# A gated delta-rule layer with experts on one core: a loop body of six chunks instead of one, squares summed on ScalarE from transposed tiles, and another order of the work

## The chip, the cores and the metric

The kernel runs on one core of a Trainium2 chip. TensorE (PE) multiplies, VectorE (DVE), ScalarE (ACT) and GpSimd (POOL) do the element-wise work, SyncE (SP) issues the DMAs. Each engine takes its own instructions in the order in which they stand; they wait for one another by semaphores. The metric is the device time of one execution in microseconds, the median of the runs shown. Data are float32; some products take rounded float32 or bfloat16 parts.

## The reference, cut to what matters

The input is 2 sequences of 2048 tokens with 256 features. Each layer norm, the attention-like part, the second norm and the experts are all computed:

```python
mixed = hidden_states @ Wqkv.T + bqkv               # 4096 channels: q 8x128, k 8x128, v 16x128
z = hidden_states @ Wz.T + bz
beta = sigmoid(hidden_states @ Wb.T + bb)
g = -exp(A_log) * softplus(hidden_states @ Wa.T + ba + dt_bias)
y = depthwise_causal_conv(mixed, conv_w, taps=4) + conv_b
q, k, v = split(silu(y))
q, k = repeat(q, 2, heads), repeat(k, 2, heads)      # 8 -> 16 heads
q = q * rsqrt(sum(q * q) + 1e-6) * 128 ** -0.5
k = k * rsqrt(sum(k * k) + 1e-6)
for t in tokens:                                     # per head, state is 128 x 128
    state = state * exp(g_t)
    delta = (v_t - k_t @ state) * beta_t
    state = state + outer(k_t, delta)
    out_t = q_t @ state
core = out * rsqrt(mean(out * out) + 1e-6) * norm_w * silu(z)
x = x + layernorm(core @ Wout.T + bout)
x = x + layernorm(shared(x_n) + top8_of_16_experts(x_n))   # x_n = layernorm(x)
```

## The kernel before, in words

The tokens are cut into 32 chunks of 128. The recurrence is taken chunk by chunk: within a chunk of a head it is a triangular system whose inverse is built (16 by 16 blocks on GpSimd, then three doubling levels on TensorE and a correction), and the state S of 128 x 128 a head is carried on. The 16 heads of a chunk go in four groups of four; **a group of a chunk is an item**, so there are 128 items. A group has two pairs of q and k tiles and four v tiles.

The work is a pipeline over items. In item w = (t, g) each engine does, in one fixed order: projection, convolution taps and SiLU of the item three ahead (a, "new"); k-q products, sums of squares, decays and the triangle of the item two ahead (f, "front"); the doubling levels of the item one ahead (v, "invert"); state products, solve and new state of w itself ("state"); gate, norm and output projection of the item before (u, "post"). Four functions more hang on certain groups: `chunk_front` makes the normed input and gates of the next chunk (groups 0 and 1), `experts` runs the expert part of the chunk before (norms in group 0; hT, ffn1, G0 in group 1; G1, G2 in group 2; G3, laT, ffo in group 3; the products D0 to D3 in between).

The order of this is written out by hand in a function `item(w, stages)` on each engine, four of them (TensorE's at L702, ScalarE's at L981, VectorE's at L1317, and those of GpSimd and SyncE). `run` calls them: t = -1 and t = 0 as straight code, t = 1 to 30 in a loop (`eng.Fori(1, chunks - 1)`, L313) whose body holds the four items of one chunk, t = 31 and 32 as straight code. Values that semaphores are waited for depend on the loop's register.

PSUM has eight banks with fixed uses: bF0 and bF1 take the projections of q, k and of v (and bF0 half of G, bF1 the gate's projection z); bQ the k-q products, the exponents and the inversion's Q; bXT the sums of squares, the transposed k, the transposed parts and the inversion's transposed X; bX v's transposes and X; bS and bD the state products, solve and new state; bB, by turns in the order of `B_ORDER`, core transposes, output projection and the experts' products.

The places that the change touches, in the order of one item on the data's way: ScalarE's `silu` makes QK; `square_qk` (L842) squares its four tiles of 128 x 128 into Sq at the end of the item; in the next item TensorE's `ss` (L492) multiplies each with a column of ones, which leaves four sums a token in bXT; VectorE's `squares` (L1138, L1140) adds the epsilon into Sse and makes Epq; `ktr` (L499), behind it on TensorE, transposes the two k tiles into the same bank, which ScalarE's `keys` (L865) copies to Kn. ScalarE's `key_norm` (L859, L861) takes logarithm and root of Sse; GpSimd makes the decay exponents with it in nine small steps (L1455 to L1471, the last write Parts); TensorE's `parts_t` (L505) transposes them, ScalarE copies (PartsT), TensorE's `exponents` (L517 to L521) spreads them over bQ, and ScalarE's `decays` (L887) makes Ex, from which GpSimd makes the triangle Ln and AT. The k-q products (`kkq`, L484) go to bQ. `correct` (L580) ends the inversion of w, `refined` (L1162) copies it to Tt, `solve` (L602) uses it. `update_s` (L1186) writes S for two heads; `ks_qs` (L594, L595) of the second pair waits for the first pair's update.

Of the kernel before, what the change touches and what calls it, by code (L numbers as in the profile page):

```python
# [39 lines left out]
P = 128  # L40
# [60 lines left out]
def layer_kernel(nc, x, wqkv, conv, wz, wba, rows, cols, wout, shared1, wlat, shared2, wup, rw, rw2,  # L101
# [6 lines left out]
    with ctx:  # L108
# [63 lines left out]
        Sq = sb("Sq", [P, 2 * GK, P])  # L172
        Sse = sb("Sse", [P, 2 * GK])
# [71 lines left out]
        def heads(bank):  # L245
# [6 lines left out]
            proj_full=2, z_full=1, kkq_full=1, ss_full=1, ktr_full=1, partsT_full=1, vtr_full=1, exp_full=1,  # L252
# [53 lines left out]
        def run(eng, item):  # L306
# [135 lines left out]
        def _(pe):  # L442
# [45 lines left out]
            def ss(f):  # L488
                pe.wait_ge(sem["xt_done"], at("xt_done", ahead(f, -2)))
                pe.wait_ge(sem["sq_done"], at("sq_done", f))  # L490
                for i in range(2 * GK):
                    last = mm(bXT[:, i:i + 1], Sq[:, i, :], ones[:, 0:1], start=True, stop=True)  # L492
                last.then_inc(sem["ss_full"], 1)

            def ktr(f):
                t, g = f
                pe.wait_ge(sem["sse_done"], at("sse_done", f))
                for kh in range(GK):
                    last = nc.tensor.transpose(heads(bXT)[:, kh, :], QK[:, g, 2 * kh + 1, :], ident)  # L499
                last.then_inc(sem["ktr_full"], 1)  # L500

            def parts_t(f):
                pe.wait_ge(sem["kn_done"], at("kn_done", f))
# [198 lines left out]
            def item(w, stages):  # L702
# [3 lines left out]
                if state:  # L706
                    ks_qs(w, 0)
                if new:
                    proj(a, 0, 0)
                if c and g == 1:  # L710
                    chunk_front(t + 1, "ba")
                if new:
                    proj(a, 0, 1)
                if front:
                    ss(f)
                if state:
                    correct(w)
                if front:
                    kkq(f)
                    ktr(f)  # L720
                if state:
                    solve(w, 0)
                if new:
                    proj(a, 1, 0)
                if front:
                    parts_t(f)
                if post:
                    core_t(u)
                if front:
                    vtr(f)  # L730
                    exponents(f)
# [3 lines left out]
                if new:  # L735
                    proj(a, 1, 1)
                if e and g == 1:
                    experts(t - 1, "hT", 0)
                if invert:
                    invert_begin(v, front)  # L740
                    invert_q(v, 0)
                if c and g == 1:
                    chunk_front(t + 1, "gc")
                if state:
                    ks_qs(w, 1)
                if e and g == 1:
                    experts(t - 1, "ffn1", 0)
                if invert:
                    invert_xt(v, 0)
                    invert_x(v, 0)  # L750
                if e and g == 3:
                    experts(t - 1, "G", 3, a if new else (chunks - 1, GROUPS - 1))
                if e and g == 2:
                    experts(t - 1, "G", 1, a if new else (chunks - 1, GROUPS - 1))
                if invert:
                    invert_q(v, 1)
                if state:
                    solve(w, 1)
                if post:
                    out_proj(u)  # L760
                if invert:
                    invert_xt(v, 1)
                    invert_x(v, 1)
                if e and g == 2:
                    experts(t - 1, "D", 1)
                if state:
                    az(w, 1)
                if invert:
                    invert_q(v, 2)
                if e and g == 1:  # L770
# [851 lines left out]
```

## Time and profile before

| what | value |
|---|---|
| median of 3 runs | 3548.47 us |
| lowest and highest | 3543.68 and 3554.87 us |
| the profiled execution's own time | 3551.05 us |
| its span, first to last instruction | 3549.2 us |
| mean granted clock of TensorE | 0.963 of 2.4 GHz |
| busy: PE, DVE, ACT, POOL | 3291.3, 2714.1, 2423.9, 2145.0 us |
| DMA | 143.89 MB, mean 41 GB/s |

How to read it: the span is one execution with a profile. Busy time of PE is modelled for pipelined products, and PEld is the load of the stationary operand that goes with each product and overlaps the one before; the distance between the starts of two PEld groups is the time that TensorE gives to the first. The slices of the page show TensorE at 90% or more from the second to the last but two, so the kernel is even over its length, and one chunk inside it can stand for all. A wait is put down to what released it; "issue" means that the profile shows nothing that did.

### The profile page before, as it was taken

The numbers are of one execution on the slowest core, as the hardware profiler recorded it, in microseconds if no ns is written. First come the engines' busy times: TensorE is split into PE (matmuls) and PEld (weight loads), VectorE is DVE, ScalarE is ACT, GpSimd is POOL, SyncE is SP. The second block draws the span as 40 slices with busy tenths as digits, with TensorE's granted clock in tenths as the row PEclk, the third lists the DMA queues.
The fourth block names the chain that finished last, engine by engine and source line by source line (L and its number), as shares of the span: only waits on it lengthen the run. The fifth ranks groups of instructions, "written<-read, shape, count | busy, mean of one in ns | idle before, by whom it ended". The sixth has DMA issues, their size and how long they took to land.

```text
span 3549.2 us, 86916 instructions
## 1 busy us (share of the span) xinstructions
PE 3291.3 (93%) x23968; PEld 2920.5 (82%) x24096; DVE 2714.1 (76%) x8720; ACT 2423.9 (68%) x5922; POOL 2145.0 (60%) x5380
## 2 busy tenths in 40 slices
PE   4999999999999999999999999999999999999986
PEld 4888888888888888888888888888888888888875
DVE  4777777877777777778787777777778777778773
ACT  3777667767767766777776777676677676677662
POOL 3766666666656656666666666666666666566660
PEclk8999999999999999999999999999999999999996
DMA  4111111111111111111111111111111111111110
GB/s 173 42 37 40 41 34 39 38 36 36 41 37 33 41 39 36 35 42 35 36 45 36 34 42 35 36 42 39 34 42 35 36 37 44 35 35 43 36 41 4
DMA packets 424188, 143.89 MB, mean 41 GB/s; under 512 B 211168, under 2 KB 421664, under 8 KB 423200
## 3 DMA queue, kind: packets, MB, share of 16 engines
q1 hardware_dynamic: 423712, 139.83, 15.1%
q14 instruction: 457, 3.74, 0.4%
q8 instruction: 19, 0.31, 0.0%
HBM read 93.11 MB, written 46.66 MB: 39 GB/s over the span
## 4 chain that ended last, share of the span: by engine, by line
PE 71%; ACT 13%; issue 8%; DVE 4%; POOL 2%; DMA 2%; DVEq 0%; SPq 0%; ACTq 0%; POOLq 0%
PE bF L464 9%; PE bB L635 6%; PE bQ L545 5%; PE bXT L553 4%; ACT L809 4%; PE bF L475 3%; PE bB L691 3%; PE bS L602 3%; PE bF L477 3%; PE bB L685 3%; PE bD L617 3%; PE bS L610 3%; PE bS L594 3%; PE bX L558 2%; PE bD L595 2%
## 5 line engine op out<-in xcount | busy, mean ns | idle before, releaser
L1103 DVE SCALAR_TENSOR_TENSOR Y<-bF,Cv,Y 128x127 f32<-128x127 f32 (+2 forms) x3072 | 852.0, 339 | 33.9 <-ACT Y L826 29.0
L464 PE MATMUL bF<-XnT,Wqkv 128*128 128x128 f32 x4096 | 556.5, 286 | 0.5 <-ACT XnT L945 0.5
L464 PEld LDWEIGHTS bF<-XnT,Wqkv 128*128 128x128 f32 x4096 | 530.1, 202 | 9.5 <-issue 2.1
L826 ACT ACTIVATE Y<-bF,Cv 128x128 f32<-128x128 f32 x1024 | 387.7, 456 | 151.4 <-PE bF L464 107.4
L896 ACT ACTIVATE XiT<-bXT 128x512 fp32r<-128x512 f32 x384 | 228.7, 596 | 296.2 <-PE bXT L553 295.1
L1531 POOL TENSOR_TENSOR Tp<-Tp 32x64 f32<-32x64 f32 (+2 forms) x768 | 361.3, 470 | 60.2
L1146 DVE TENSOR_TENSOR Qi<-bQ,Cf 128x512 fp32r<-128x512 f32 x384 | 264.0, 687 | 97.6 <-PE bQ L545 96.4
L809 ACT ACT_TABLE_LOAD x257 | 329.7, 1283 | 5.4 <-PEq L1615 0.7
L553 PE MATMUL bXT<-Qi,Xi 128*128 128x128 f32 x1536 | 301.9, 319 | 2.4 <-DVE Qi L1146 2.4
L553 PEld LDWEIGHTS bXT<-Qi,Xi 128*128 128x128 f32 x1536 | 222.1, 192 | 96.2 <-DVE Qi L1146 47.3
L1524 POOL TENSOR_TENSOR Tp<-Yb,Tm 32x64 f32<-32x64 f32 (+1 forms) x384 | 276.9, 721 | 30.1
L1524 POOL TENSOR_TENSOR Tp<-Cb,Yb 32x64 f32<-32x64 f32 (+1 forms) x384 | 274.0, 713 | 32.7 <-POOL Yb L1533 5.0
L1425 POOL TENSOR_TENSOR Ln<-Ex,KKQ 128x512 f32<-128x512 f32 x128 | 163.9, 1281 | 209.5 <-ACT Ex L887 140.3
L1539 POOL TENSOR_TENSOR Yb<-Cb,Cf 32x8 fp32r<-32x8 f32 x128 | 25.6, 200 | 392.6 <-DMA Cb<-DL 392.6
L545 PE MATMUL bQ<-XiT,LnR 128*128 128x128 f32 x1536 | 240.7, 280 | 19.4 <-ACT XiT L896 19.4
L545 PEld LDWEIGHTS bQ<-XiT,LnR 128*128 128x128 f32 x1536 | 211.8, 191 | 47.6 <-ACT XiT L896 28.7
L635 PE MATMUL bB<-Wout,CoT 128*128 128x256 f32 x1024 | 244.2, 382 | 0.9 <-ACT CoT L932 0.8
L1169 DVE SCALAR_TENSOR_TENSOR R<-bS,Sc,Vs 128x128 f32<-128x128 f32 x512 | 154.2, 342 | 98.5 <-issue 77.7
L903 ACT ACTIVATE Xi<-bX 128x512 fp32r<-128x512 f32 x384 | 226.4, 590 | 2.8 <-PE bX L564 2.3
L1458 POOL TENSOR_TENSOR HG<-LnbG,Lnk 128x4 f32<-128x4 f32 x128 | 25.7, 201 | 325.2 <-ACT Lnk L859 325.2
L635 PEld LDWEIGHTS bB<-Wout,CoT 128*128 128x128 f32 x1024 | 186.2, 192 | 21.4 <-ACT CoT L932 1.1
L602 PE MATMUL bS<-R,Tt 128*128 128x128 f32 x1024 | 179.3, 301 | 22.9 <-DVE Tt L1162 22.8
(198 smaller groups left out, 9272.2 us busy)
## 6 DMA issues: line engine op xcount, KB each, us to landing
DL<-Ln SPq DMA_DIRECT2D x128, 256.0 KB, 2.2
XiT<-DX SPq DMA_DIRECT2D x128, 256.0 KB, 2.8
Xi<-DX SPq DMA_DIRECT2D x128, 256.0 KB, 3.2
DX<-Yb SPq DMA_DIRECT2D x256, 32.0 KB, 1.8
Xf<-x SPq DMA_DIRECT2D x32, 128.0 KB, 3.2
Wqkv<-wqkv SPq DMA_DIRECT2D x4, 1024.0 KB, 17.1
Cb<-DL SPq DMA_DIRECT2D x128, 32.0 KB, 1.9
Xr<-x SPq DMA_DIRECT2D x32, 128.0 KB, 2.9
```

The costliest lines, as they stand in the source:

```text
L464: last = mm(bank[:, i, :], Wqkv[:, k, c:c + P], XnT[:, k, :], start=(k == 0), stop=(k == KT - 1))
L545: last = mm(heads(bQ)[:, h, :], LnR[:, h, :], XiT[:, h, :], start=True, stop=True)
L553: last = mm(heads(bXT)[:, h, :], Xi[:, h, :], Qi[:, h, :], start=False, stop=True, skip_group_check=True)
L602: last = mm(heads(bS)[:, i, :], Tt[:, 2 * p + i, :], R[:, i, :], start=True, stop=True)
L635: last = mm(bB[:, 0:HID], CoT[:, h, :], Wout[:, g * GH + h, :], start=(h == 0), stop=(h == GH - 1))
L809: nc.scalar.add_instruction(mybir.InstLoadActFuncSet(name=nc.get_next_instruction_name(), act_func_set_id=TABLES[name], engine=mybir.Engin ...
L826: last = op(Y[:, tile, :], bank[:, i, :], ACT.Identity, scale=c[:, TAPS - 1:TAPS], bias=c[:, TAPS:TAPS + 1])
L896: op(XiT[:, :, :], heads(bXT), ACT.Copy).then_inc(sem["xt_done"], 1)
L1103: last = stt(y, bank[:, i, 0:P - shift], Cv[:, g * TILES + tile, n:n + 1], y, ALU.mult, ALU.add)
L1146: tt(Qi[:, :, :], heads(bQ), level, ALU.mult).then_inc(sem["q_done"], 1)
L1524: then(tt(view(Tp[:, :], p * m ** 3, [[m * m, m], [m, m], [1, m]]), pair(left, p), pair(right, p), ALU.mult))
L1531: then(tt(lo, lo, hi, ALU.add))
```

## The change

Four edits.

- **The loop's body** holds six chunks (24 items) and is run 5 times, instead of one chunk run 30 times. `chunks - 2` is 30, and six is the first of 6, 5, 3, 2, 1 that divides it. In the built program TensorE's body has 3814 instructions instead of 647, ScalarE's 1697 instead of 283, VectorE's 2236 instead of 393, GpSimd's 2015 instead of 345.
- **Sums of squares**: `ss` is gone, and so is the squaring of QK as a whole at the end of `activated`. `ktr` transposes all four tiles, q and k, and waits for SiLU and for the bank. At the head of the item ScalarE squares each transposed tile from PSUM and sums it along the free axis with the instruction's accumulator into Ssq. `squares` on VectorE reads Ssq. `parts_t`, which overwrites the bank, waits for the squares too.
- **The order** of the items is written anew on TensorE, ScalarE and VectorE.
- `B_ORDER` has gc ahead of hT.

```diff
-            with eng.Fori(1, chunks - 1) as t:
-                for g in range(GROUPS):
-                    item((t, g), "cafispe")
+            steps = next(n for n in (6, 5, 3, 2, 1) if (chunks - 2) % n == 0)
+            with eng.Fori(0, (chunks - 2) // steps) as i:
+                for k in range(steps):
+                    for g in range(GROUPS):
+                        item((i * steps + k + 1, g), "cafispe")
...
-            def ss(f):
-                pe.wait_ge(sem["xt_done"], at("xt_done", ahead(f, -2)))
-                pe.wait_ge(sem["sq_done"], at("sq_done", f))
-                for i in range(2 * GK):
-                    last = mm(bXT[:, i:i + 1], Sq[:, i, :], ones[:, 0:1], start=True, stop=True)
-                last.then_inc(sem["ss_full"], 1)
-
             def ktr(f):
                 t, g = f
-                pe.wait_ge(sem["sse_done"], at("sse_done", f))
-                for kh in range(GK):
-                    last = nc.tensor.transpose(heads(bXT)[:, kh, :], QK[:, g, 2 * kh + 1, :], ident)
+                pe.wait_ge(sem["xt_done"], at("xt_done", ahead(f, -2)))
+                pe.wait_ge(sem["silu_done"], at("silu_done", f, 1))
+                for i in range(2 * GK):
+                    last = nc.tensor.transpose(heads(bXT)[:, i, :], QK[:, g, i, :], ident)
                 last.then_inc(sem["ktr_full"], 1)
...
             def square_qk(f):
-                act.wait_ge(sem["silu_done"], at("silu_done", f, 1))
-                act.wait_ge(sem["ss_full"], at("ss_full", ahead(f, -1)))
-                op(Sq[:, :, :], QK[:, f[1], :, :], ACT.Square).then_inc(sem["sq_done"], 1)
+                act.wait_ge(sem["ktr_full"], at("ktr_full", f))
+                act.wait_ge(sem["sse_done"], at("sse_done", ahead(f, -1)))
+                for i in range(2 * GK):
+                    last = op(Sq[:, i, :], heads(bXT)[:, i, :], ACT.Square, accum_out=Ssq[:, i:i + 1])
+                last.then_inc(sem["sq_done"], 1)
...
-                dve.wait_ge(sem["ss_full"], at("ss_full", f))
+                dve.wait_ge(sem["sq_done"], at("sq_done", f))
                 dve.wait_ge(sem["lnk_done"], at("lnk_done", ahead(f, -1)))
-                ts(Sse[:, :], bXT[:, 0:2 * GK], L2_EPS, None, ALU.add).then_inc(sem["sse_done"], 1)
+                ts(Sse[:, :], Ssq[:, :], L2_EPS, None, ALU.add).then_inc(sem["sse_done"], 1)
...
                 if front:
-                    ss(f)
+                    kkq(f)
...
+                if e and g == 3:
+                    experts(t - 1, "D", 2)
```

TensorE at the head of an item, here group 0, before (lines with ISA or REGISTER_ALU only set up waits and are left out by the dots; S are the state products, Wqkv the projections, Sq the sums of squares, bX<-Xi,Qi the correction):

```order
...
L594 MATMUL bS<-S,QK 128x256
L595 MATMUL bD<-S,QK 128x256
...
L464 MATMUL bF<-XnT,Wqkv 128x128 x8
...
L492 MATMUL bXT<-Cf,Sq 128x1 x4
...
L580 MATMUL bX<-Xi,Qi 128x128 x4
...
L484 MATMUL bQ<-QK 128x256 x2
L499 MATMUL bXT<-Cf,QK 128x128 x2
...
L602 MATMUL bS<-R,Tt 128x128 x2
L464 MATMUL bF<-XnT,Wqkv 128x128 x4
...
L505 MATMUL bXT<-Ch,Parts 128x128
```

And now:

```order
...
L592 MATMUL bS<-S,QK 128x256
L593 MATMUL bD<-S,QK 128x256
...
L487 MATMUL bQ<-QK 128x256 x2
...
L467 MATMUL bF<-XnT,Wqkv 128x128 x4
...
L496 MATMUL bXT<-Cf,QK 128x128 x4
L578 MATMUL bX<-Xi,Qi 128x128 x4
L467 MATMUL bF<-XnT,Wqkv 128x128 x4
...
L467 MATMUL bF<-XnT,Wqkv 128x128 x4
...
L600 MATMUL bS<-R,Tt 128x128 x2
L467 MATMUL bF<-XnT,Wqkv 128x128 x4
...
L503 MATMUL bXT<-Ch,Parts 128x128
```

The k-q products moved ahead of the projections, the transposes ahead of the correction, and all four parts of the projection now stand before the transposed parts; in groups 2 and 3 a product D stands before and behind the correction besides.

ScalarE at the head of the same item, before:

```order
...
L859 ACTIVATE Lnk<-Sse 128x2
L861 ACTIVATE Rki<-Lnk 128x2
...
L826 ACTIVATE Y<-bF,Cv 128x128 x4
L865 ACTIVATE Kn<-bXT 128x256
...
L910 ACTIVATE Qg<-bD,Sc 128x128 x2
L915 ACTIVATE Z<-bS 128x256
L874 ACTIVATE PartsT<-bXT 128x128
```

And now:

```order
...
L840 ACTIVATE Sq,Ssq<-bXT 128x128 x4
...
L908 ACTIVATE Qg<-bD,Sc 128x128 x2
...
L857 ACTIVATE Lnk<-Sse 128x2
L859 ACTIVATE Rki<-Lnk 128x2
...
L823 ACTIVATE Y<-bF,Cv 128x128 x4
L863 ACTIVATE Kn<-bXT 128x256
L913 ACTIVATE Z<-bS 128x256
L872 ACTIVATE PartsT<-bXT 128x128
```

The four squares and the scaling of the queries now stand ahead of the key norms.

VectorE in the same item, before (Y the taps, O and S the updates):

```order
...
L1138 TENSOR_SCALAR Sse<-bXT 128x4
L1140 TENSOR_SCALAR Epq<-Sse 128x2
...
L1162 COPY Tt<-bX 128x512
...
L1103 SCALAR_TENSOR_TENSOR Y<-bF,Cv,Y 128x127 x4
...
L1103 SCALAR_TENSOR_TENSOR Y<-bF,Cv,Y 128x126 x4
L1178 TENSOR_TENSOR O<-Qg,bS 128x256
L1186 SCALAR_TENSOR_TENSOR S<-S,Sc,bD 128x128 x2
...
L1103 SCALAR_TENSOR_TENSOR Y<-bF,Cv,Y 128x125 x4
```

And now:

```order
...
L1137 TENSOR_SCALAR Sse<-Ssq 128x4
L1139 TENSOR_SCALAR Epq<-Sse 128x2
...
L1161 COPY Tt<-bX 128x512
...
L1102 SCALAR_TENSOR_TENSOR Y<-bF,Cv,Y 128x127 x4
...
L1102 SCALAR_TENSOR_TENSOR Y<-bF,Cv,Y 128x126 x4
...
L1102 SCALAR_TENSOR_TENSOR Y<-bF,Cv,Y 128x125 x4
L1177 TENSOR_TENSOR O<-Qg,bS 128x256
L1185 SCALAR_TENSOR_TENSOR S<-S,Sc,bD 128x128 x2
```

The third set of taps moved ahead of the updates of O and S.

## Rows read from the trace of the kernel before

**Rows 1.** The page, busy us, share of the span, instructions of each engine.

```profile
PE 3291.3 (93%) x23968; PEld 2920.5 (82%) x24096; DVE 2714.1 (76%) x8720; ACT 2423.9 (68%) x5922; POOL 2145.0 (60%) x5380
```

**Rows 2.** Windows: stretch, its us, busy us of each engine, PEclk, DMA.

```profile
199.08:224.82 25.74, 23.80 (x168) 20.84 (x169) 21.53 (x77) 18.21 (x50) 17.00 (x43) 1.00 0.17 43
224.82:250.78 25.96, 25.55 (x201) 23.34 (x201) 20.68 (x73) 18.91 (x48) 16.62 (x43) 1.00 0.14 36
250.78:276.63 25.85, 25.66 (x206) 23.11 (x205) 19.80 (x60) 19.37 (x46) 16.64 (x43) 1.00 0.14 36
...
1026.98:1058.34 31.36, 28.05 (x187) 24.61 (x187) 22.30 (x66) 19.07 (x46) 16.67 (x43) 0.89 0.15 39
1058.34:1082.91 24.57, 23.07 (x167) 20.23 (x166) 21.55 (x78) 18.36 (x51) 16.89 (x43) 1.00 0.16 42
...
3387.80:3413.24 25.44, 25.03 (x187) 22.07 (x187) 21.88 (x66) 18.63 (x47) 16.72 (x43) 1.00 0.16 41
```

**Rows 3.** SyncE's stores of results, instructions of the loop, first and last start.

```profile
L394 SPq MOVE out<-Yo x30: 29/29/29, 297.0 to 3407.7; - x30
```

**Rows 4.** Waits: us in total, times, longest us.

```profile
DVE R L1169 <- issue: 77.7, 29, 3.1
...
PE bXT L499 <- DVE Sse L1138: 65.3, 29, 2.6
```

**Rows 5.** Windows behind the jump at 1046 us, columns as above.

```profile
1050.00:1052.00 2.00, 2.00 (x9) 2.00 (x10) 1.51 (x5) 1.09 (x4) 1.71 (x9) 0.50 0.08 18
```

**Rows 6.** Timeline, TensorE's loads in an item's head: start, us, engine, line.

```profile
1016.39 0.42 PEld L594 LDWEIGHTS bS<-S,QK 128*128 128x128 f32 x2
...
1017.27 1.97 PEld L464 LDWEIGHTS bF<-XnT,Wqkv 128*128 128x128 f32 x16
...
1019.16 0.97 PEld L492 LDWEIGHTS bXT<-Cf,Sq 128*128 128x128 f32 x8
...
1020.05 0.53 PEld L580 LDWEIGHTS bX<-Xi,Qi 128*128 128x128 f32 x4
...
1020.50 0.74 PEld L484 LDWEIGHTS bQ<-QK 128*128 128x128 f32 x4
...
1021.26 0.36 PEld L499 LDWEIGHTS bXT<-Cf,QK 128*128 128x128 f32 x2
...
1021.58 0.53 PEld L602 LDWEIGHTS bS<-R,Tt 128*128 128x128 f32 x4
...
1023.03 0.42 PEld L624 LDWEIGHTS bB<-Cf,O 128*128 128x128 f32 x4
...
1026.30 0.19 PEld L535 LDWEIGHTS bXT<-XiT,IdR 128*128 128x128 f32 x1
```

**Rows 7.** Timeline, the other engines in the same stretch.

```profile
1016.82 0.69 DVE L1148 TENSOR_TENSOR Qi<-bQ,Cf 128x512 fp32r<-128x512 f32 x1 [0.64 <-PE bQ L573]
...
1020.26 0.16 DVE L1138 TENSOR_SCALAR Sse<-bXT 128x4 f32<-128x4 f32 x1 [2.23 <-PE bXT L492]
...
1020.76 0.69 DVE L1162 COPY Tt<-bX 128x512 f32<-128x512 f32 x1
...
1020.83 1.50 ACT L826 ACTIVATE Y<-bF,Cv 128x128 f32<-128x128 f32 x4
...
1022.23 0.20 POOL L1471 TENSOR_TENSOR Parts<-HGf,Cf 128x8 bf16<-128x8 f32 x1
...
1022.48 0.65 ACT L910 ACTIVATE Qg<-bD,Sc 128x128 f32<-128x128 f32 x2
...
1023.10 2.26 DVE L1103 SCALAR_TENSOR_TENSOR Y<-bF,Cv,Y 128x127 f32<-128x127 f32 x8
...
1025.71 0.61 DVE L1186 SCALAR_TENSOR_TENSOR S<-S,Sc,bD 128x128 f32<-128x128 f32 x2
```

**Rows 8.** Groups of ScalarE by form: busy us, mean ns, idle before.

```profile
L859 ACT ACTIVATE Lnk<-Sse 128x2 f32<-128x2 f32 x128 | 25.5, 200 | 106.4 <-DVE Sse L1138 105.2
...
L977 ACT ACTIVATE LaT<-bB 128x128 f32<-128x128 f32 x32 | 8.9, 277 | 26.1 <-PE bB L695 26.1
```

More of the change, by code:

```diff
@@ L707, in item @@
                     ks_qs(w, 0)
+                if front:
+                    kkq(f)
                 if new:
                     proj(a, 0, 0)
[L710 to L711 removed]
+                if front:
+                    ktr(f)
+                if e and g == 2:
+                    experts(t - 1, "D", 0)
+                if state:
+                    correct(w)
+                if e and g == 3:
+                    experts(t - 1, "D", 2)
                 if new:
                     proj(a, 0, 1)
[L714 to L720 removed]
+                    proj(a, 1, 0)
                 if state:
@@ L734, in item @@
                     new_state(w, 0)
-                if new:
-                    proj(a, 1, 1)
+                if c and g == 1:
+                    chunk_front(t + 1, "gc")
+                if invert:
+                    invert_begin(v, front)
+                    invert_q(v, 0)
+                if state:
+                    ks_qs(w, 1)
                 if e and g == 1:
@@ L985, in item @@
                 if front:
+                    square_qk(f)
+                if state:
+                    query_state(w, 0)
+                if front:
                     key_norm(f)
@@ L1015, in item @@
                     experts(t - 1, "G", 1)
+                if e and g == 1:
+                    experts(t - 1, "ffn1", 0)
+                if state:
+                    query_state(w, 1)
+                    solved(w, 1)
                 if invert:
                     inverse(v, 0)
-                if state:
-                    solved(w, 1)
                 if c and g == 0:
@@ L1038, in item @@
                     experts(t - 1, "laT", 0)
+                if e and g == 2:
+                    experts(t - 1, "G", 2)
                 if new:
@@ L1322, in item @@
                     right_side(w, 0)
-                if e and g == 2:
-                    experts(t - 1, "D", 0)
-                if front:
-                    squares(f)
-                if new:
-                    ended(a)
-                if state:
-                    refined(w)
                 if post:
@@ L1333, in item @@
                 if front:
+                    squares(f)
+                if state:
+                    refined(w)
+                if new:
+                    ended(a)
+                if e and g == 3:
+                    experts(t - 1, "D", 2)
+                if e and g == 1:
+                    experts(t - 1, "hn", 0)
+                if front:
                     products(f)
+                if new:
+                    taps(a, 0, 2)
                 if c and g == 1:
                     chunk_front(t + 1, "sp")
+                if e and g == 2:
+                    experts(t - 1, "D", 0)
                 if new:
-                    taps(a, 0, 2)
                     taps(a, 0, 1)
-                if e and g == 1:
-                    experts(t - 1, "hn", 0)
+                    taps(a, 0, 0)
                 if state:
@@ L1344, in item @@
                     update_s(w, 0)
+                if c and g == 0:
+                    chunk_front(t + 1, "norm")
                 if new:
-                    taps(a, 0, 0)
                     tails_out(a, 0)
+                if invert:
+                    mask_q(v, 0)
                 if c and g == 1:
                     chunk_front(t + 1, "gc")
-                if invert:
-                    mask_q(v, 0)
-                if c and g == 0:
-                    chunk_front(t + 1, "norm")
+                if new:
+                    first_tokens(a, 0)
                 if state:
```

141 lines of the change are left out of this document (61 added, 80 removed), and 4 rows, old and new, of the table B_ORDER.

## The prediction

> **What bounds the kernel now.** I read the page first: TensorE is busy 93% of the span [rows 1], the others 60 to 76%, so the first question is where TensorE does not do useful work. The means of the page hide that, so I cut the span into items (four make a chunk of 128 tokens) at the DMA that carries an item's triangle out, and asked for the busy time of each stretch [rows 2]. Three kinds of stretch appear. In straight code (the first pass through the loop's body, the way out of the loop, and all items that lie inside an iteration) an item takes 25.44 to 25.96 us and the granted clock is 1.00. A stretch with the jump back to the top of the body in it takes 31.36 us, at a mean clock of 0.89, and the item behind it is a little shorter, 24.57 us. Three stretches of the first iteration, 25.74, 25.96 and 25.85, and the way out of the loop, 25.44, are together a chunk without a jump: 102.99 us. The iterations as they are: the stores of the results run from 297.0 to 3407.7 us in 30 iterations [rows 3], so 3110.7 / 29 = 107.27 us each.
>
> The difference, 4.28 us, is the price of one jump. The waits show its parts: 29 times VectorE stood before its first instruction of the body, 77.7 / 29 = 2.7 us, with nothing that released it; 29 times TensorE then waited for VectorE, 65.3 / 29 = 2.3 us [rows 4]. Behind that pause the granted clock is 0.50 (1.2 instead of 2.4 GHz) for some microseconds [rows 5]. A part of the loss is caught up in the next item, which is why I take the period and not the single stretch: 31.36 - 25.44 would say 5.9.
>
> Within straight code TensorE is the bound almost alone. Interval less busy time in the four stretches is 0.41 + 1.94 + 0.41 + 0.19 = 2.95 us of 102.99 [rows 2]. So its work is 100.0 us a chunk, and its stalls 3.
>
> **The change, part by part. The body of six chunks** removes jumps: 29 before, 4 after (5 iterations). 25 x 4.28 = 107 us. What each engine issues for a chunk stays about the same, and the straight parts of before show that code without a jump is supplied in time. A remark on the four that stay: the trace shows that TensorE itself began the next body without a pause at the jump (it waited only for VectorE), with a body of 647 instructions. The Trainium skill (Runtime: NRT & Kernel Launch, Instruction fetch mechanics) gives TensorE room for 2048 instructions and says that a taken branch to a target outside what is held stalls for a fetch. The new body has 3814 on TensorE, so by the page its jump would stall too; if that costs what VectorE's does, 4 x 2.7 = 11 us more, an estimate that no run here shows yet and that the sum leaves out.
>
> **Sums of squares.** On TensorE the four products with a column of ones go: they hold its load slot from 1019.16 to 1020.05, 0.89 us. The two transposes of k (1021.26 to 1021.58, 0.32) become four; four such transposes are 0.42 in the row of L624 [rows 6]. Gain 0.89 + 0.32 - 0.42 = 0.79 us an item, 3.1 a chunk: work 100.0 - 3.1 = 96.9 us. VectorE now reads four numbers a partition from SBUF instead of PSUM, which I cost at nothing.
>
> On ScalarE one squaring of 512 columns, off the path at the end of an item, becomes four of 128 columns read from PSUM with an accumulator, and they stand at the head of the item behind the transposes, on the path to the key norms. No row has the accumulator. The nearest rows are four instructions of 128 columns from PSUM in 1.50 us (L826) [rows 7] and one alone in 0.28 (L977) [rows 8]. From below 4 x 0.28 = 1.1 us; from above 1.5 plus 0.2 each if reading the accumulator is a small instruction of its own (a logarithm of two columns is 200 ns) [rows 8], 2.3. I take 1.5, the row with the same shape and source. The Trainium skill (ScalarE: Activation LUTs, What ACT_TABLE_LOAD costs) would have an instruction without pointer operands at 186 + 107 ns and 93 ns of overlap, so 0.9 us for the four, an estimate; the chain below would then be 0.6 us shorter in each item.
>
> **The order.** I walk the head of the new order with the durations of the old one, from the load of the state products at 1016.39 as zero [rows 6, 7]. TensorE: state products to 0.88. Then the k-q products, which stood behind ss: they write bQ, which VectorE's last mask of the item before must have read, and that ended at 1017.51, +1.12. So they start at 1.2 (**stall 0.3**) and end at 1.96 (0.76 long). One half of a projection (0.95) to 2.9, four transposes to 3.3. ScalarE can square from about 3.5 (a reader followed the last load by 0.2 at ss, 1020.05 to 1020.26) to 5.0; Sse at 5.2; Tt, 0.5 behind it in the old order and 0.4 in the new, from 5.6 to 6.3. TensorE meanwhile has the correction (0.45) and two halves (1.89): 5.65. In items 0 and 1 of a chunk it then waits for Tt until 6.35 (**stall 0.7**). In items 2 and 3 the products D stand there as cover and hide it. Key norms, exponents: from Sse to the last Parts were 2.17 us (1020.26 to 1022.43); ScalarE's scaling of the queries (L910, 0.65) now stands in front of the key norms, so they come at 5.2 + 2.17 + 0.45 = 7.8 (0.2 of the 0.65 run while Sse is made), and TensorE is there at 7.75; it waits a little for them, and again for ScalarE's copy, which has four taps (1.50) in front: **stall 0.35** together. Head: 1.35 us in items 0 and 1, 0.65 in 2 and 3.
>
> What comes later: the taps of q and k begin when ScalarE has done query scaling, key norms (two small ones, 0.45) and its own four taps, 5.0 + 0.65 + 0.45 + 1.5 = 7.6; before they began at 6.7 (1023.10). The new order puts all three sets (2.26 / 2 = 1.13 each) ahead of the update of O and S, before it was two. So S is updated at 7.7 + 3.4 + 0.4 + 0.6 = 12.1; before 1026.32, +9.9. TensorE's head took 9.91 (to the load at 1026.30), now 9.9 - 0.8 + 1.35 = 10.5 (much the same in items 2 and 3, where the products D fill the gap); with two copies into PSUM and the first inversion product, 0.9, it stands before the second pair of state products at 11.4 and waits for S: **stall 0.7** in every item. Queued behind that wait is all of the inversion chain.
>
> Sum of the walk for a chunk: 2 x 1.35 + 2 x 0.65 + 4 x 0.7 = 6.8 us. Of today's 3 us the order should take away the wait before the turned blocks, since z's second half now lies in between, and leave about 0.9: 7.7 us. That is a ceiling for the price of 1.5 us, since in it every engine keeps its old lateness, while ScalarE, with 19 of 25.9 us busy [rows 2], would be ahead by what it no longer does at the item's end. The floor is today's 3 us. A chunk is then 96.9 + 3.0 = 99.9 to 96.9 + 7.7 = 104.6 us, against 102.99. I take the middle, 102.3, because the two ends are worth the same to me: - 0.7 us a chunk.
>
> **Sum**, on the profiled execution's span of 3549.2 us, with 31 chunks' worth of full items: 3549.2 - 107 - 31 x 0.7 = 3420. The run lay 1.85 us above its span (3551.05), and 2.6 above the median of the three runs, so on the median's scale this is 3420 less 1: **about 3420 us**.
>
> **The rivals.** (a) The order hides its own waits, and all the work taken from TensorE is time: 99.9 us a chunk, 3549 - 107 - 31 x 3.1 = 3346. For it: VectorE stands 2.23 us waiting for ss in the item shown [rows 7], so there is slack to reorder in; against it the walk above. (b) The walk in full: 104.6 us a chunk, + 1.6 x 31 = 50, so 3492. For it: the S update and Tt are hard dependencies of the same item. (c) Slower than before: the accumulating squares are dear. They lie on the chain transposes, squares, Sse, Tt, taps, S, so each 0.1 us of them is 0.1 an item, 0.4 a chunk. With the walk in full the whole gain is gone when a chunk is 102.99 + 107 / 31 = 106.4 us, that is 1.8 / 4 = 0.45 us an item over the walk: squares of 1.95 us for the four. At the upper bound of 2.3 it is 0.8 an item, 107.8 a chunk: 3442 + 149 = 3591. (d) The jumps left become dearer, or more of the loss is recovered today than I see: at most some 10 to 20 us; it goes into the range. (e) The change does nothing for the jumps, because the straight code is not fed in time: then 29 stretches at 0.89 would be replaced by pauses elsewhere. The first iteration and the prologue speak against it, 0.02 of chance.
>
> **How the numbers follow.** Middle case, 3375 to 3460: 0.45. (a), 3335 to 3375, and somewhat under it where today's 3 us shrink too: 0.24. (b), 3460 to 3535: 0.20. (c) with (e): 0.11, of which 0.08 ends beyond + 0.3%, the rest within. A measurement of this kernel can tell about 0.3%, 10.6 us, from no change: that is 3538 to 3559. So faster 0.88, same 0.04, slower 0.08. For 8 in 10 the range takes in (a), the middle and the most of (b): 3335 to 3515.
>
> **What would show it.** Right for the jump: 4 times instead of 29 an unreleased pause of VectorE at the head of the body, the clock at 1.00 between, and straight items. Right for the squares: their four near 1.5 us, starting at 3.5 after the item's start. Right for the walk: waits of the solve for Tt and of the second state products for S in most items; if they are absent, (a) holds. Wrong: squares over 1.9 us, a chunk inside the body longer than 103 us with TensorE's idle time ahead of the solve or the state products, or a clock that falls within the body because those stalls add up.

## The result and the profile after

| | before | after |
|---|---|---|
| median | 3549.74 us (4 runs) | 3455.02 us (4 runs) |
| lowest and highest | 3543.68, 3554.87 | 3447.76, 3462.44 |
| profiled execution, its span | 3551.05, 3549.2 us | 3456.82, 3455.0 us |
| mean granted clock | 0.963 | 0.980 |

The ratio is 0.9736, 95% interval 0.9722 to 0.9751: 2.6% faster, 95 us between the medians. The forecast was 3420 us, with a range of 3335 to 3515.

The page of the changed kernel, to set beside [rows 1]:

```profile
span 3455.0 us, 84800 instructions
...
PE 3197.1 (93%) x23200; PEld 2796.3 (81%) x23328; DVE 2756.8 (80%) x8720; ACT 2502.6 (72%) x6818; POOL 2151.3 (62%) x5380
```

TensorE has 768 products fewer (1024 of `ss` gone, 256 transposes more), ScalarE 896 instructions more, seven an item. Four squares instead of one are only three of them; the other four are read-outs of the accumulator (below).

The windows, cut at the same DMA as [rows 2]: first the stretch with a jump, then the four items of a straight chunk behind it.

```profile
792.94:825.06 32.12, 26.42 (x183) 23.11 (x182) 22.14 (x66) 19.51 (x54) 16.67 (x43) 0.95 0.16 41
825.06:849.96 24.90, 22.70 (x156) 19.47 (x158) 22.23 (x74) 19.08 (x57) 17.20 (x43) 1.00 0.17 43
849.96:876.20 26.24, 25.61 (x196) 22.95 (x195) 21.69 (x75) 19.53 (x55) 16.67 (x43) 1.00 0.14 35
876.20:902.16 25.96, 25.37 (x198) 22.41 (x198) 19.73 (x61) 19.98 (x53) 16.67 (x43) 1.00 0.15 36
902.16:927.76 25.60, 24.33 (x179) 21.44 (x179) 21.67 (x65) 19.23 (x54) 16.71 (x43) 1.00 0.18 46
```

This straight chunk takes 102.70 us (102.6 to 103.8 in the others, 102.9 in the mean; one, with an item of 28.9 us, takes 105.2) and TensorE is idle for 0.6 to 2.2 us in each item, 4.7 in the chunk. There are four stretches with a jump, 31.60 to 32.68 us long. What happens at one, in the timeline:

```profile
812.30 0.59 PE L592 MATMUL bS<-S,QK 128*128 128x256 f32 x2 [4.32 <-issue]
...
813.56 0.61 DVE L1168 SCALAR_TENSOR_TENSOR R<-bS,Sc,Vs 128x128 f32<-128x128 f32 x2 [2.79 <-PE bS L592]
...
817.29 0.28 ACT L840 ACTIVATE Sq<-bXT 128x128 f32<-128x128 f32 x1 [6.74 <-PE bXT L496]
```

Now TensorE itself stands 4.32 us with nothing that releases it, and the others wait for it. In the kernel before, TensorE went on into the next body and VectorE was the one that paused [rows 4].

The waits of TensorE's loads, longest first (us in total, times, longest):

```profile
PEld bXT L551 <- DVE Qi L1145: 72.3, 111, 1.5
PEld bB L693 <- issue: 51.7, 32, 2.7
PEld bS L592 <- DVE S L1185: 49.8, 119, 1.0
...
PEld bX L578 <- ACT Xi L901: 23.0, 33, 1.8
...
PEld bX L562 <- ACT XiT L894: 13.2, 31, 1.5
PEld bQ L487 <- ACT VT L834: 11.8, 30, 0.4
PEld bS L600 <- DVE Tt L1161: 10.6, 34, 1.8
```

The wait for S is there in 119 of 128 items. The wait for Tt, for which the prediction took 0.7 us in half of the items, is small.

Last the head of an item of group 3 in the timeline, to set beside [rows 6, 7]. Its zero, the load of the state products, is 890.52:

```profile
890.52 0.42 PEld L592 LDWEIGHTS bS<-S,QK 128*128 128x128 f32 x2
...
891.76 0.73 PEld L487 LDWEIGHTS bQ<-QK 128*128 128x128 f32 x4 [0.40 <-ACT VT L834]
...
893.51 0.47 PEld L496 LDWEIGHTS bXT<-Cf,QK 128*128 128x128 f32 x4
...
894.26 0.28 ACT L840 ACTIVATE Sq<-bXT 128x128 f32<-128x128 f32 x1 [0.30 <-PE bXT L496]
894.43 0.19 ACT L840 ACTIVATION_READ_ACCUMULATOR Sq<-bXT 128x1 f32 x1
...
894.52 0.27 ACT L840 ACTIVATE Sq<-bXT 128x128 f32<-128x128 f32 x1
```

And further on in the same item:

```profile
895.27 0.64 ACT L908 ACTIVATE Qg<-bD,Sc 128x128 f32<-128x128 f32 x2
...
895.43 0.17 DVE L1137 TENSOR_SCALAR Sse<-Ssq 128x4 f32<-128x4 f32 x1 [0.79 <-ACT Sq L840]
...
898.08 3.42 DVE L1102 SCALAR_TENSOR_TENSOR Y<-bF,Cv,Y 128x127 f32<-128x127 f32 x12 [0.62 <-ACT Y L823]
...
901.75 0.60 DVE L1185 SCALAR_TENSOR_TENSOR S<-S,Sc,bD 128x128 f32<-128x128 f32 x2
...
902.46 0.30 PEld L592 LDWEIGHTS bS<-S,QK 128*128 128x128 f32 x2 [0.34 <-DVE S L1185]
```

The k-q products start at +1.24, the squares at +3.74 and end at +4.75 (the next instruction starts at 895.27): 1.0 us for four. S is updated at +11.83 and the second state products start at +11.94, behind a wait.

### The profile page after: what moved, and what is told of

It is laid out like the page before. It is cut to its first block, busy times and chain, and to the rows that moved or that the text cites. A ratio compares the mean times of both kernels' runs of the same rounds, so it can differ in the third digit from the quotient of the medians.

```text
span 3455.0 us, 84800 instructions
## 1 busy us (share of the span) xinstructions
PE 3197.1 (93%) x23200; PEld 2796.3 (81%) x23328; DVE 2756.8 (80%) x8720; ACT 2502.6 (72%) x6818; POOL 2151.3 (62%) x5380
## 4 chain that ended last, share of the span: by engine, by line
PE 52%; DVE 19%; ACT 10%; issue 7%; POOL 7%; DMA 4%; POOLq 0%; SPq 0%; DVEq 0%; ACTq 0%
DVE Y L1102 10%; PE bF L467 5%; PE bB L633 5%; ACT Y L823 5%; PE bB L683 4%; PE bB L689 3%; PE bXT L551 3%; PE bS L592 3%; PE bQ L487 3%; PE bF L480 3%; PE bX L556 2%; PE bQ L569 2%; PE bQ L543 2%; POOL Tp L1524 2%; PE bD L593 2%
## 5 line engine op out<-in xcount | busy, mean ns | idle before, releaser
L467 PE MATMUL bF<-XnT,Wqkv 128*128 128x128 f32 x4096 | 530.4, 278 | 0.0
L467 PEld LDWEIGHTS bF<-XnT,Wqkv 128*128 128x128 f32 x4096 | 503.2, 194 | 7.2
L551 PE MATMUL bXT<-Qi,Xi 128*128 128x128 f32 x1536 | 266.8, 296 | 39.3 <-DVE Qi L1145 39.3
L551 PEld LDWEIGHTS bXT<-Qi,Xi 128*128 128x128 f32 x1536 | 215.5, 193 | 80.3 <-DVE Qi L1145 72.3
L1203 DVE SCALAR_TENSOR_TENSOR O<-O,Fr,Gz 128x128 f32<-128x128 f32 x512 | 154.7, 363 | 101.6 <-ACT Fr L925 101.6
L592 PE MATMUL bS<-S,QK 128*128 128x256 f32 x512 | 163.5, 401 | 53.2 <-DVE S L1185 36.3
```

The source lines that it names most:

```text
L467: last = mm(bank[:, i, :], Wqkv[:, k, c:c + P], XnT[:, k, :], start=(k == 0), stop=(k == KT - 1))
L551: last = mm(heads(bXT)[:, h, :], Xi[:, h, :], Qi[:, h, :], start=False, stop=True, skip_group_check=True)
L592: mm(bS[:, 0:2 * P], QK[:, g, 2 * p + 1, :], s, start=True, stop=True).then_inc(sem["ks_full"], 1)
```

## The experiments

Twelve kernels, each timed 4 to 10 times beside the kernel before on the same chip. That one took 3546.7 us beside e1 to e4, 3552.1 beside e5 to e8, 3548.2 beside e9 to e11 and 3549.4 beside e12. A difference between two kernels of different groups is therefore uncertain by about 5 us; the ratios, which take this out, are given where it matters.

| kernel | body | squares | order | us | ratio to before (95%) |
|---|---|---|---|---|---|
| changed | 6 | new | new | 3455.0 | 0.9736 (0.9722, 0.9751) |
| e1 | 6 | old | old | 3422.2 | 0.9656 (0.9640, 0.9672) |
| e2 | 1 | new | new | 3619.2 | 1.0211 (1.0194, 1.0228) |
| e3 | none | new | new | 3421.5 | 0.9647 (0.9631, 0.9664) |
| e4 | 3 | new | new | 3482.2 | 0.9826 (0.9810, 0.9842) |
| e5 | 6 | new | old | 3555.5 | 1.0014 (1.0004, 1.0025) |
| e6 | 6 | old | new | 3602.5 | 1.0133 (1.0116, 1.0150) |
| e7 | none | old | old | 3407.4 | 0.9592 (0.9576, 0.9608) |
| e8 | 6 | new | new, S earlier | 3553.4 | 0.9998 (0.9989, 1.0008) |
| e9 | 1 | old | old, shifted | 3554.7 | 1.0017 (1.0008, 1.0027) |
| e10 | 1 | new | new, shifted | 3534.2 | 0.9955 (0.9937, 0.9972) |
| e11 | 6 | new | old, Tt first | 3540.7 | 0.9981 (0.9970, 0.9992) |
| e12 | 6 | new and two more | new | 3502.9 | 0.9868 (0.9850, 0.9885) |

### The loop alone, and the rest alone

e1 is the kernel before with

```diff
-            with eng.Fori(1, chunks - 1) as t:
-                for g in range(GROUPS):
-                    item((t, g), "cafispe")
+            with eng.Fori(0, (chunks - 2) // 6) as i:
+                for k in range(6):
+                    for g in range(GROUPS):
+                        item((i * 6 + k + 1, g), "cafispe")
```

> The kernel before with the six-chunk body alone; squares and order stay old. Theory: the whole gain of the change comes from the jumps, 29 before and 4 now. 25 x 4.28 = 107 us go, and the four that stay cost some 2.3 us more each, since TensorE's body of six chunks is long and TensorE itself now pauses at the jump (4.3 us before the state products in the changed kernel): 3549 - 107 + 9 = 3451, that is the changed kernel's time within 10 us. Rival: the new squares and order carry a part of the gain (the prediction gave them 22 us, its first rival 96); then this kernel is slower than the changed one by as much, 3477 or more.

> The changed kernel with a body of one chunk again: new squares and new order, 29 jumps. Theory: squares and order are worth nothing together, 3549 within 10 us, and a straight chunk inside takes 103 us as before. Rival: they gain 22 us (3527) or they lose (the chain behind the accumulating squares makes a jump dearer: 29 x 2 = 58 us more, 3600).

Both theories missed, and e2 lies 19 us above even its rival's 3600. The loop alone takes 124.5 us off, more than the whole change, so the new squares and the new order lose 33 us in the six-chunk body (28 by the ratios). In a body of one chunk they lose 72, for a reason that e10 below shows. Nothing of the gain of the whole change is theirs.

The windows of e1 for a straight chunk show what an undisturbed old chunk is:

```profile
918.99:943.28 24.29, 22.85 (x165) 19.95 (x164) 20.97 (x77) 18.02 (x49) 17.07 (x43) 1.00 0.17 43
943.28:970.01 26.73, 26.05 (x203) 23.64 (x202) 22.59 (x74) 19.24 (x49) 16.68 (x43) 1.00 0.14 35
970.01:995.83 25.82, 25.71 (x207) 23.08 (x205) 19.76 (x60) 19.37 (x46) 16.56 (x43) 1.00 0.15 36
995.83:1021.32 25.49, 25.16 (x189) 22.12 (x187) 22.04 (x66) 18.73 (x47) 16.75 (x43) 1.00 0.18 47
```

The four make 102.33 us (101.3 to 102.9 in the straight chunks of the trace, about 102.1 in the mean), with TensorE busy for 99.8 and idle for 2.6. The changed kernel's chunk of 102.70 has it busy for 98.0 and idle for 4.7. So the work did shrink, by 1.8 us in the modelled busy time, and idle time grew by 2.1. Over all straight chunks of the two traces the difference is larger than in this pair, 102.9 against 102.1.

### The price of a jump

e3 is the changed kernel with `for t in range(1, chunks - 1)` in place of the loop, e7 the same of the kernel before, e4 the changed kernel with three chunks in the body.

> The changed kernel without a loop, all chunks as straight code, so no jump. Stretches with a jump take 31.6 to 32.7 us in the changed kernel's trace against 25.6 of the same item without, 6.6 us each; four of them are 26 us. Theory: 3455 - 26 = 3429. Rival: the waits on constants instead of registers make the engines issue faster too, and it gains more than 35 us; or straight code of this length is not fetched in time, and it gains nothing.

> The kernel before, all chunks as straight code, old squares and old order. With the six-chunk body a stretch with a jump took 29.5 to 30.0 us instead of 25.5, 4.2 us each, and there are four: 3422 - 17 = 3405. In the changed kernel going straight gave 33 us for four jumps of 6.6, so 8 more than the jumps; if that is due to waits on constants and holds here too: 3397. Rival: it stays at 3422.

> The changed kernel with a body of three chunks, 9 jumps instead of 4. TensorE's body is then about 1900 instructions. Theory, after the Trainium skill (Runtime: NRT & Kernel Launch, Instruction fetch mechanics), by which TensorE holds 2048: TensorE does not pause at the jump by itself, a jump costs about what it did in the kernel before, 4.3 us, so 3455 - 26 + 9 x 4.3 = 3468, and no wait of 4 us without a releaser stands before TensorE's first state products. Rival: the price of a jump comes from the new form and not from the body's length, 6.6 us each: 3455 + 5 x 6.6 = 3488.

Without a loop the changed kernel gains 33 us for its four jumps (the windows would give 26; the straight chunks of e3 are also 0.3 us shorter, 102.6 to 102.7), the old one 15 for its four, as its theory had it (23 by the ratios; the windows of e1 give 16). Straight code of all chunks is fetched in time. **e7, the old squares in the old order as straight code, is the fastest kernel of the study: 3407 us, 4.1% under the kernel before.** e4's time lies between its two expectations, 27 us above the changed kernel for five jumps more. Its trace decides for the rival: the chunks with one of its nine jumps take 109.5 us against 103.0 for the others, 6.5 a jump, as in the changed kernel (109.4 against 102.9), and the first chunks of e4, ahead of the loop, happen to be 5 us shorter. TensorE did pause in it, nine times, 38.0 us in all:

```profile
PE bS L592 <- issue: 38.0, 9, 4.4
```

The length of the body therefore isn't what separates a TensorE that pauses from one that doesn't: e2, whose body is as short as in the kernel before, pauses at all 29 jumps. The page shows what goes with it. It lists the packets of each instruction queue. These are the rows for TensorE's queue, of the kernel before, of e2 and of the changed kernel:

```profile
q8 instruction: 19, 0.31, 0.0%
```

```profile
q8 instruction: 279, 4.57, 0.5%
```

```profile
q8 instruction: 210, 3.44, 0.4%
```

There were 19 packets of 16 KB in the kernel before, fewer than its 29 jumps: TensorE's loop body was not fetched again. In e2 it was fetched anew in each iteration, nine packets each. (All of the code as straight code, e3, is 195 packets. The changed kernel has 15 more and e4, with five jumps more, another ten, so two for each jump.) The instructions recorded for a chunk are about 1500 on TensorE in the trace (a float32 product is two loads and two products there), not the 647 of the built program. The prediction compared that 647 with the 2048 of the Trainium skill (Runtime: NRT & Kernel Launch, Instruction fetch mechanics). With a body of this size the position of the code may decide, which can be tried by moving the code without changing it:

```diff
             pe.wait_ge(early, 16 * len(EARLY))
+            for _ in range(128):
+                pe.wait_ge(setup, SETUP)
             run(pe, item)
```

> The kernel before with 128 instructions more on TensorE ahead of everything, each a wait that is already fulfilled; nothing else. In the kernel before TensorE's instruction queue (q8) moved 19 packets of 16 KB in all, so its body was not fetched again in 29 jumps; in the new order with a one-chunk body, which has 11 instructions fewer, it moved 279, and TensorE paused 4.3 us at each jump. Theory: where the body begins within the fetched blocks decides, and a shift by half a block makes this body too be fetched again: 200 packets or more, pauses of TensorE at 29 jumps, and a time 20 to 50 us over the kernel before. Rival: position plays no part (the body's own form does), and it stays at 3549 with some 20 packets.

> The changed kernel with a one-chunk body (3619) and the same 128 fulfilled waits ahead on TensorE. Theory of the position: its body falls inside what is held, q8 shows some 20 packets instead of 279, the pause of 4.3 us at 29 jumps goes, and with it up to 29 x 2.5 = 70 us, 3550 to 3590. Rival: 3619 and 279 packets again.

e10 is 85 us faster than e2 through 128 instructions that do nothing, and below its expected 3550 to 3590. Its queue shows 19 packets again, and TensorE's pause before the state products is gone; VectorE is the one that pauses, as in the kernel before. So e2's loss comes from the repeated fetch: with the body held in both, the new squares and order in a one-chunk body are 14 us faster than the kernel before (ratio 0.9955). Their straight chunks are longer there too, but a chunk with a jump takes 106.8 us in the mean, against 107.3. The queue and VectorE's wait in e10:

```profile
q8 instruction: 19, 0.31, 0.0%
```

```profile
DVE R L1168 <- issue: 79.1, 29, 3.1
```

e2, for comparison:

```profile
PE bS L590 <- issue: 124.3, 29, 5.6
```

e9 shows no such effect, 19 packets and 3554.7 us, as its rival had it; of the 6.5 us over the kernel before, 3.7 are the shift itself (the first triangle leaves at 58.64 instead of 54.95 us). So position decides in the new form, and this one shift does not push the old body out. Where the edge lies for it was not tried.

The granted clock adds to the price of a jump. Windows of 2 us (columns as in [rows 2]) just behind TensorE's pause, first of the changed kernel, which paused for 4.32 us, then of e1, which paused for 2.14:

```profile
814.00:816.00 2.00, 2.00 (x10) 1.82 (x9) 1.22 (x5) 0.00 (x0) 0.00 (x0) 0.50 0.05 12
```

```profile
804.00:806.00 2.00, 2.00 (x20) 1.97 (x19) 0.97 (x2) 1.31 (x5) 0.35 (x2) 1.00 0.20 25
```

TensorE is busy through both, in the first at the lower level (0.50, 1.2 GHz) and in the second at the upper (2.4 GHz). e10 shows what the lower one costs, since its jumps are of both kinds: the stretch with the jump takes 30.4 us in the mean where the clock fell behind the jump (17 times) and 28.6 where it did not (12 times), with TensorE's waits in it the same, 4.0 us in both kinds. The clock fell behind each of the changed kernel's four jumps, for 3.4 to 6.8 us, and behind one of e1's, for 3.4 us, whose stretch was no longer than the others. A stretch at the lower level leaves half of its time undone, so by estimate it is 2.1 us a jump in the changed kernel and 0.4 in e1. That is the larger part of what separates their prices, 6.4 and 4.1 us by the chunk period.

### Squares and order apart

e5 has the new squares in the old order (six-chunk body), e6 the old squares in the new order: `ss` where the four transposes stood, the two of k behind the correction.

> The old order with the six-chunk body and the new squares: four transposes stand where ss stood, the squares at the head of ScalarE's item before the key norms. The loop alone gave 3422, the whole change 3455, so squares and order lose 33 us together. Theory O (the order loses, because it puts three sets of taps before the update of S and the k-q products before what hides their wait): this kernel keeps the 3422 of the loop alone or gains up to 30 us, since TensorE has 3.1 us less work a chunk. Theory S (the squares on the path lose): it falls to about 3455.

> The new order with the six-chunk body and the old squares: one squaring of 512 columns at the end of the item, ss where the four transposes stood, two transposes behind the correction. Theory O: about the changed kernel's 3455, or up to 50 us above it, since TensorE's work comes back. Theory S: 3422 or less.

Neither theory holds, since both expected the parts to add. The squares alone cost 133 us (3422 to 3555), the order alone 180 (to 3602), and together they cost 33 (127, 169 and 28 by the ratios): each costs far less in the other's company. e5's waits show where its time goes:

```profile
DVE Sse L1137 <- ACT Sq L840: 325.4, 128, 5.4
...
PEld bS L600 <- DVE Tt L1161: 213.9, 118, 2.6
```

VectorE stands at the sums of squares in all 128 items, the copy to Tt is queued behind, and TensorE waits for that, 1.7 us an item. The new order spends its two early halves of a projection on exactly this place, and there the wait is 10.6 us in all in the changed kernel. e11 takes the queue away instead:

```diff
+                if state:
+                    refined(w)
                 if front:
                     squares(f)
                 if new:
                     ended(a)
-                if state:
-                    refined(w)
```

> Old order, six-chunk body, new squares (3555, TensorE 214 us waiting for Tt), with one move on VectorE: the copy to Tt stands ahead of the sums of squares, so it is not queued behind the wait for ScalarE's squares. Theory: 133 us of loss against the old squares come from this queue in the first place; the wait for Tt goes, and the next late thing is the transposed parts, 1.3 us an item by the prediction's walk (2.17 from Sse to Parts plus 1.0 of squares against 2.6 of cover), less 0.8 of work: 3422 + 128 x 0.5 = 3486. Rival: the length of the chain sets the item however it is queued, and it stays within 15 us of 3555.

It gained 15 us of the 133 (12 by the ratios), so the rival holds. The wait for Tt fell from 213.9 to 39.1 us and another has its place, a few instructions on, in e11:

```profile
PEld bXT L503 <- POOL Parts L1470: 188.6, 120, 2.3
```

That speaks for the length of the chain from the squares through the key norms and GpSimd as what sets the item in the old order, with the queue deciding only which instruction shows it. e11's expectation had put this wait at 1.3 us, although the terms that it gives, 2.17 + 1.0 - 2.6, come to 0.6; it is 1.6 in 120 items.

The granted clock has a part in both losses. Between 100 and 3300 us of the trace, e1 has one stretch at the lower level, 3.4 us long, and the changed kernel six, 27 us in all. e5 has 16 with 68 us and e6 has 32 with 123 us, most of them inside the body and not at a jump. Half of that time, less e1's, is by estimate 32 us of the 133 in e5 and 60 of the 180 in e6. At one place in e5's chunk 8 items with such a stretch take 26.7 us in the mean and 21 without take 25.3, with the same 3.2 us of waits of TensorE in both. Which wait of e6 brings its stretches on was not tried; no experiment separates the rest of its loss either.

### One move, and the squares' own price

e8 puts the first pair's updates of O and S back before the third set of taps.

> The changed kernel with one move on VectorE: the updates of O and S for the first pair stand before the third set of taps again, as in the old order. In the changed kernel's trace the second pair's state products wait for S 119 times, 0.3 to 0.55 us each with TensorE idle. Theory: the wait is on the path, it goes, and 0.4 us an item or 1.6 a chunk come back: 3455 - 45 = 3410. Rival: the third set of taps, now later, makes the gate projection or the next mask wait as long, and it stays within 10 us of 3455.

It lost 98 us, and both expectations missed. The wait for S went, but VectorE now reaches the update before TensorE has the product for it and stands idle, 64.0 us in 103 waits where the changed kernel has 9.6 in 6, and what is queued behind it comes later. TensorE's wait for the first mask doubles from the 72.3 us above. The two rows are e8's:

```profile
PEld bXT L551 <- DVE Qi L1145: 155.6, 171, 2.1
```

```profile
DVE O L1177 <- PE bS L608: 64.0, 103, 4.5
```

These waits are not all of it. e8's granted clock falls inside straight code, about once a chunk: 27 stretches and 109 us at the lower level against the changed kernel's 6 and 27, by estimate 41 of the 98 us. The items show it: at the place in the chunk where most of these stretches lie, 22 items with one take 27.4 us in the mean and 7 without 25.4, with the same 2.7 us of waits of TensorE in both. At one of them TensorE had waited 1.4 us for the first mask, with no jump near:

```profile
952.00:954.00 2.00, 1.08 (x9) 1.09 (x10) 1.97 (x8) 0.39 (x1) 0.00 (x0) 1.00 0.20 36
954.00:956.00 2.00, 2.00 (x12) 1.82 (x11) 1.97 (x7) 1.78 (x7) 1.00 (x5) 0.66 0.11 17
956.00:958.00 2.00, 2.00 (x7) 1.55 (x6) 1.39 (x6) 0.00 (x0) 1.53 (x7) 0.50 0.00 0
```

e12 adds two squares ahead of the four.

```diff
+                for i in range(GK):
+                    op(Sq2[:, i, :], heads(bXT)[:, i, :], ACT.Square, accum_out=Ssq2[:, i:i + 1])
                 for i in range(2 * GK):
```

> The changed kernel with two squares more (of the first two tiles, into tiles that nothing reads) ahead of the four, 0.26 us each by the starts in the changed kernel's trace, so 0.5 us more between the transposes and Sse in every item. Theory, as the prediction had it: the squares lie on the path of the item, each 0.1 us of them is near 0.1 us an item: 3455 + 128 x 0.5 = 3519, a little less where other work of VectorE comes later anyway, 3500 to 3520. Rival: after the new order there is slack behind the squares, and it stays within 10 us of 3455.

It costs 48 us for 0.52 us more an item, within its theory's range: 72% of it reaches the end. The squares are on the path in the changed kernel too. Its time at the lower clock is the changed kernel's, 27 us, so the clock has no part in this loss.

## Why the prediction was right or wrong

The time fell in the stated range and in its middle case, 3375 to 3460. By its own steps that is in part luck: two terms were wrong by 18 and by 55 us, in opposite directions. The jumps gave 124.5 us and not 107; squares and order lost 33 and did not gain 22. 3420 - 18 + 55 = 3457, against 3455 measured.

**The jumps: mechanism right, price too low.** 29 became 4, the straight stretches run at a clock of 1.00. Priced at 4.28 us each they were to give 107; alone they gave 124.5 (e1), 5.0 each. The term that was too low rests on the straight chunk of 102.99 us: it was put together from the first iteration, whose first stretch of 25.74 us [rows 2] is not typical. e1 has 24.3 to 24.6 there in nearly every straight chunk, 102.1 in all, and 107.27 - 102.1 = 5.2 is the right price. The prediction also read the 24.57 us behind the jump as loss caught up; that item is as short where there is no jump.

**The jumps that stay.** The sum left out that they may become dearer. In the changed kernel they cost 6.4 us each (109.4 less 102.9) against 4.1 in e1 (106.2 less 102.1); the difference comes with TensorE's longer pause, 4.2 us against 2.1, and the lower clock behind it. The remark drawn from the Trainium skill (Runtime: NRT & Kernel Launch, Instruction fetch mechanics) did foretell that TensorE would pause, and four pauses of 4.2 us are there; but its reason, 3814 instructions against 2048, was counted on the wrong number, and e2 pauses with the short body. The Trainium skill's rule in the same section, that a target outside what is held must be fetched, is borne out by the packet counts of e2 and e10, 279 and 19.

**TensorE's work: right in kind.** Predicted 3.1 us a chunk less, 1.8 in the modelled busy time.

**The squares: mis-sized, and below the stated range.** 1.5 was taken, 1.1 to 2.3 given; they take 1.0. The read-out of the accumulator is an instruction of its own, as the upper bound supposed, but it runs beside the next square, so that one follows another by 0.26 us. The estimate of 0.9 us for the four that the prediction worked out from the Trainium skill (ScalarE: Activation LUTs, What ACT_TABLE_LOAD costs) was the nearer one. Rival (c), slower through dear squares, had the right chain: e12's 0.72 us per microsecond stands against its assumption of 1.

**The walk: the places right.** Start of the k-q products 1.2 (1.24 measured), of the squares 3.5 (3.74), end of the S update 12.1 (11.83). The stall before the second state products is there, 0.42 us each in 119 items, where 0.7 in every item was predicted. That for Tt is 10.6 us in 34 waits and not 0.7 in half the items; the squares, 0.5 us shorter than taken, can account for a part of this; the rest is not shown. Instead of it came waits that the walk did not see: for the first mask (72.3 us against 47.8 in e1), before the transposed expert sum L693 (51.7, 28.2 in e1), and at the correction for ScalarE's X (23.0), which now stands behind two norms.

**Stalls against work: the balance was wrong.** The middle of floor and ceiling gave - 0.7 us a chunk. Measured it is 102.9 against 102.1, + 0.8 and so 25 us in 31 chunks, and 33 in the whole with the four dearer jumps. In length the chunk was near the middle case's 102.3. As a change, which is what the sum used, the walk in full was nearer: + 1.6 against the old chunk as the prediction read it. Its reason for going lower, that ScalarE would be ahead by what it no longer does at the item's end, was argued and no run shows it. e8 shows that the place of one step on VectorE is worth 98 us. That stalls inside the body can bring the lower clock with them stood among the signs of being wrong; it is what e5, e6 and e8 do, and the changed kernel hardly does.

What stays open: which waits bring the clock down and which do not, since items of e8 and e5 with equal waits are of both kinds; why TensorE pauses for 4.2 us at a jump of the changed kernel and for 2.1 in e1 (8.5 us in 4), although both fetch its body again; what makes e6 lose the most; and by how much the old body would have to be shifted to be fetched again.

## What to carry to other kernels

A loop's jump has a price that no instruction shows: cut the trace into periods with and without it, and take several straight periods, not the first. Look at the granted clock in fine windows as well, inside the body too. If the code can be straight, that alone may be worth more than a better body: here it gave 4.1%, while the body with less work for TensorE made the straight chunk longer. The order and the durations that it is fitted to belong together: changed alone, the squares lost 133 us and the order 180, and both together 33. So try the parts apart, and beside the loop alone, before keeping them.

## What the runs showed of the hardware

- TensorE's instructions come by a queue of their own in packets of 16 KB. A loop body of some 1500 recorded matmul and load instructions was fetched once (19 packets in all) or in every iteration (279), depending on where it lies: 128 idle instructions ahead of it (e10 against e2) were worth 85 us over 29 jumps.
- At a jump the first instruction of the body stood unreleased for 2.7 us on VectorE in the kernel before, 2.1 us (e1) to 4.3 us (e2) on TensorE where its body had to be fetched again.
- Behind TensorE's pauses of 3.8 to 4.6 us at the changed kernel's four jumps the granted clock was 0.50 for 3.4 to 6.8 us each time; behind those of 2.0 to 2.3 us in e1 it was 1.00 three times of four. It fell inside straight code as well, once a chunk in e8, where a stretch of 3.4 us at the lower level went with an item longer by 1.4 us (e5) or 2.0 us (e8) at equal waits.
- Summing with ScalarE's accumulator makes a second instruction, 0.21 us long, that lies beside the next one: four squares of 128 columns from PSUM took 1.0 us with their read-outs (the changed kernel at 894.26 us).
